# Attention scores as eight 64x32 matmuls a product instead of two of 64x128

## What is computed

```python
h = _layernorm(x) * (1 + ca) + sa
xh = h.reshape(1, 4096, 16, 16)                       # 16 heads of 16 features
q = einsum('bnhd,hed->bnhe', xh, Wq)
scores = einsum('bnhe,bmhe->bhnm', q, q) / NORM       # 4096 x 4096 per head
attn = softmax(scores, axis=-1)
res = einsum('bhnm,bmhe->bnhe', attn, q)
x = x + ga * (res.reshape(1, 4096, 256) @ Wp.T + bp)
h = _layernorm(x) * (1 + cb) + sb
x = x + gb * ffn(h)     # layernorm, 256 -> 1024, silu, 1024 -> 256, residual
```

## Time and profile before

| | before |
|---|---|
| median of 3 runs | 1982.75 us (1982.64 to 1982.96) |
| the profiled execution | 1984.1 us |
| its span (first to last instruction) | 1982.3 us |
| TensorE / ScalarE / VectorE / GpSimd busy | 94% / 95% / 75% / 68% |
| mean granted TensorE clock | 0.996 |

### The profile page before, as it was taken

One profiled execution on the slowest core, in us unless ns is written; L12 is line 12 of the kernel. 1 busy time (PEld: TensorE's weight loads), 2 busy tenths in 40 slices (PEclk: granted clock), 3 DMA queues, 4 the chain that ended last, 5 costly groups with the idle time before them and its releaser, 6 DMA issues.

```text
span 1982.3 us, 47924 instructions
## 1 busy us (share of the span) xinstructions
PE 1872.9 (94%) x18453; PEld 547.5 (28%) x18453; DVE 1482.4 (75%) x2599; ACT 1882.3 (95%) x1491; POOL 1353.1 (68%) x2265
## 2 busy tenths in 40 slices
PE   8787889999999999999999999999999999999999
PEld 6311112222222222222222222222222222322225
DVE  5578677778777777777777787777777777777763
ACT  5898999999999999999999999999999999999992
POOL 5277777478746787477774787557874777747870
PEclk9899999999999999999999999999999999999999
DMA  6531112112111222211212212111121121211100
GB/s 202 164 98 43 39 46 48 48 53 52 49 45 46 53 53 54 53 43 44 57 49 53 54 43 56 41 52 53 44 63 45 41 52 52 55 35 39 43 12 13
DMA packets 121394, 108.43 MB, mean 55 GB/s; under 512 B 21952, under 2 KB 120128, under 8 KB 120912
## 3 DMA queue, kind: packets, MB, share of 16 engines
q1 hardware_dynamic: 120416, 103.69, 19.6%
q10 hardware_dynamic: 752, 1.67, 0.2%
HBM read 96.49 MB, written 8.65 MB: 53 GB/s over the span
## 4 chain that ended last, share of the span: by engine, by line
PE 52%; ACT 28%; issue 8%; DVE 6%; POOL 3%; POOLq 0%; DVEq 0%
PE attend_sums L919 26%; ACT attend_probs L866 17%; PE attend_scores L905 15%; ACT attend_probs L872 10%; PE attend_out L927 8%; PE attend_scores L927 1%; DVE attend_spare L1123 1%; DVE attend_probs L1117 1%; DVE attend_probs L1116 1%; ACT hidden L860 1%; PE attend_out L933 1%; DVE attend_spare L1125 1%; PE attend_sums L933 0%; POOL attend_spare L832 0%; POOL attend_spare L834 0%
## 5 line engine op out<-in xcount | busy, mean ns | idle before, releaser
L866 ACT ACTIVATE attend_probs<-attend_scores 128x2048 f32<-128x2048 f32 x683 | 1287.1, 1884 | 21.5 <-PE attend_scores L905 20.9
L919 PE MATMUL attend_sums<-attend_probs,values 128*17 128x512 f32 x8192 | 1007.0, 597 | 14.6 <-DVE attend_att L1093 6.8
L1116 DVE COPY attend_probs<-attend_scores 128x896 f32<-128x896 f32 x620 | 675.3, 1089 | 345.1 <-PE attend_scores L905 340.3
L872 ACT ACTIVATE attend_probs<-attend_probs 128x896 f32<-128x896 f32 (+1 forms) x682 | 659.5, 967 | 12.3 <-DVE attend_probs L1116 11.2
L905 PE MATMUL attend_scores<-asks,keys 64*128 64x512 f16 x4096 | 565.3, 381 | 78.8 <-ACT attend_probs L866 70.5
L830 POOL TENSOR_TENSOR attend_spare<-attend_spare 128x256 f32<-128x256 f32 x310 | 204.2, 659 | 291.9 <-DVE attend_spare L1125 291.4
L905 PEld LDWEIGHTS attend_scores<-asks,keys 64*128 64x128 f16 x4096 | 149.2, 94 | 672.4 <-ACT attend_probs L866 514.0
L919 PEld LDWEIGHTS attend_sums<-attend_probs,values 128*17 128x17 f32 x8192 | 174.7, 96 | 522.4 <-issue 466.4
L834 POOL TENSOR_TENSOR attend_spare<-attend_spare 128x256 f32<-128x256 f32 x310 | 240.5, 776 | 25.8
L837 POOL TENSOR_TENSOR attend_spare<-attend_spare,attend_probs 128x256 f32<-128x256 f32 x310 | 227.6, 734 | 25.9
L839 POOL TENSOR_TENSOR attend_probs<-attend_spare 128x256 f32<-128x256 f32 x310 | 227.6, 734 | 24.3
(11 more groups left out here) (162 smaller groups left out, 834.8 us busy)
## 6 DMA issues: line engine op xcount, KB each, us to landing
keys<-parts_dram SPq DMA_DIRECT2D x768, 64.0 KB
keys<-parts_dram SPq DMA_DIRECT2D x256, 56.0 KB
asks<-parts_dram SPq DMA_DIRECT2D x192, 64.0 KB
start_x_in<-L_attn_x SPq DMA_DIRECT2D x8, 512.0 KB, 9.5
parts_dram<-start_q_parts SPq DMA_DIRECT2D x16, 256.0 KB, 2.7
attend_x_now<-L_attn_x SPq DMA_DIRECT2D x8, 512.0 KB, 4.4
out<-base SPq DMA_DIRECT2D x15, 256.0 KB, 2.6
asks<-parts_dram SPq DMA_DIRECT2D x64, 56.0 KB
```

Of the source, the lines that this page charges most:

```text
L866: act.activation(place(n, 2), ps_scores[:, 0:4, :], ACT.Exp, scale=scale).then_inc(exps_done, 1)
L872: act.activation(cols, cols, ACT.Exp, scale=scale).then_inc(exps_done, 1)
L919: last = pe.matmul(ps_sums[32 * hq:32 * hq + E1, :], values[:, j + STEPS * b, (gg % Q_GROUPS) * Q_HEADS + hq, :], place(gg * PAIRS + Q_HEA ...
L1116: dve.tensor_copy(flat(n, 0, DIRECT), bank[:, 0:DIRECT]).then_inc(copied, 1)
```

## The change

Each of the two matmuls of a product, with 64 rows and 128 columns, is made as four of 64 rows and 32 columns. Column tile q takes 32 of the 128 keys, and writes partitions 32q to 32q + 31 of the same PSUM bank. The four column tiles are the outer loop and the two row halves the inner one, so a product is eight matmuls in eight tiles. Waits, semaphores and everything else are unchanged, and so are the values that are written.

```diff
-                    for b in range(2):
-                        rows, col = slice(64 * b, 64 * b + 64), (j % K_STEPS) * P
-                        last = pe.matmul(ps_scores[:, 2 * i + b, :], keys[rows, part % K_RING, hq, col:col + P],
-                                         asks[rows, group * Q_HEADS + hq, :], start=True, stop=True)
+                    for q in range(4):
+                        for b in range(2):
+                            rows, col = slice(64 * b, 64 * b + 64), (j % K_STEPS) * P + 32 * q
+                            last = pe.matmul(ps_scores[32 * q:32 * q + 32, 2 * i + b, :], keys[rows, part % K_RING, hq, col:col + 32],
+                                             asks[rows, group * Q_HEADS + hq, :], start=True, stop=True)
                     last.then_inc(scores_ready, 1)
```

## The result

| | before | after |
|---|---|---|
| median us | 1982.7 (1982.45 to 1982.96, 4 runs) | 1996.65 (1995.37 to 1997.16, 4 runs) |
| ratio, 95% interval | 1 | 1.0069 (1.0052 to 1.0087) |
| the profiled execution: time, span | 1984.1, 1982.3 | 1995.37, 1993.6 |

The change made the kernel 14 us slower. The forecast was 33 us slower, 2016: the right way, inside the range, and more than twice too much.

The account below looks back on a forecast made before the run. ScalarE and TensorE bound the kernel in a loop of 2.61 us a round. Skew 0.04 plus later end 0.03, less 0.015 covered, times 626 rounds adds 34 us to 1984.1: 2016 us at the median, range 1962 to 2050.

Parts of the forecast that it names:

- The loop: Wide exp, two scores products, next wide exp: 2.61 us a round, to grow by 0.07, of which 0.015 is covered.
- point 1: Scores matmuls: row halves and column tiles were taken to overlap fully, so a product stays at 0.22 us.
- point 2: Inside a scores product: eight tiles start one after another, so the last starts 0.04 us later.
- point 3: Scores to their reader: column tiles finish 0.03 us later than recorded.
- point 4: TensorE's switches between scores and sums: stops of 0.09 and 0.12 us, 0.23 us a round in all, were taken to stay.
- Rival 1: The stops go because only columns count; TensorE's round becomes 2.44 us, the time 1971 us; chance 0.29.
- point 5: Fetching 24,576 more instructions, some 4.1 MB in the queue, costs nothing because it is hidden behind matmuls.
- The tanh rounds: The 56 rounds with a tanh between the exps: 3.12 us each, with 0.5 us to spare against a later product.
- The sum: Loop growth of 0.07 us, less 0.015 covered, gives 0.055 in each of 626 rounds: 34 us.

Follow-up runs that it names:

- third_product_second: Kernel before, with the third product made between the first and second in 640 of 683 rounds, same matmuls; 2055.69 us, 1.0364 of the kernel before.
- two_column_tiles: Each scores product made as four matmuls in tiles of 64 x 64, where the kernel before has two; 1990.53 us, 1.0035 of the kernel before.
- one_shape_at_a_time: Kernel before plus four extra fp16 matmuls a round, tiles varied so type, rows and columns change one at a time; 2181.55 us beside 1983.44.
- split_queries: Each scores product made as eight matmuls of 64 rows x 128 columns over 128 queries, without column tiles; 1990.57 us, 1.0037 of the kernel before.
- half_outer: The change with its loops exchanged, row half outer and column tile inner; 1995.47 us, 1.0066 of the kernel before.

## Why the prediction was right in kind and wrong in size

- *The loop.* Right: it sets the round of the change, and third_product_second, which ends the second product 0.2 later with the same instructions, has a round 0.19 longer. The 0.015 us of cover stood in the forecast without a working; by the parts above the loop of before is 2.58 and the cover is 0.02. TensorE's own round was said to grow by the same 0.07, in step with the loop; it grew by 0.02, to 2.611 or 2.617, since only the skew is in it.
- *Streaming* (point 1). Right: eight tiles of 64 x 32 stream together, and products start 0.22 to 0.23 apart.
- *Skew* (point 2). This step failed: 0.04 was taken, 0.02 measured. I took the 0.006 a step from the fp32 column tiles; the row halves' 0.003 to 0.004, the lower bound in the text, was the right row. (The 0.045 of the upper end has no row; by point 2 it is 0.042 less 0.004, and the bound some 4 us lower.)
- *The later end* (point 3). Right: 0.03 (0.441 against 0.412 from the last matmul to its reader), and two_column_tiles shows that it grows with the column tiles. The two rows that it was taken from have different readers, ScalarE and VectorE; with ScalarE as the reader of both (line 506's, and line 882) it is 0.037 and 0.067, the same 0.03.
- *The stops* (point 4). Right that they stay, and one_shape_at_a_time shows that a change of rows alone is enough, which the forecast could only argue. Rival 1 is out.
- *Instructions* (point 5). Right in the fetching: 4.01 MB where 4.1 was said. That so many cost nothing is not shown: split_queries, with as many, loses half of what the change loses, by a TensorE round that is 0.02 longer.
- *The tanh rounds.* A tanh round was read as 3.12 us with 0.5 to spare. The trace of before has a median of 3.43 us for the 56: in 33 of them TensorE has 16 sums and 8 matmuls of line 927, and ScalarE waits for it (fence below). So these had nothing to spare, and the 56 together paid 1.4 us.
- *The sum.* This step failed too, and it is the larger lesson. It added 0.055 us to each of 626 rounds. But a longer loop is a floor under the round, not an addition to it: a round that was already longer pays nothing until the floor reaches it. Of the 626 rounds without a tanh in the trace of before, 454 were shorter than 2.63 us. Raising just these to 2.63 gives 11.9 us; measured in the profiles are 11.5 us in the rounds without a tanh and 1.4 in those with one, together the 12.9 above. Round by round, these 454 got 12.5 us longer from before to after and the 172 others 1.0 shorter. With the forecast's own floor of 2.655 the same count gives 23 us instead of 34. So of the 22 us too much in the profile (34 against 12), some 11 are the sum, and some 11 the floor that was 0.025 too high, of which the skew is 0.02 and the cover 0.005. By the same count TensorE's own round of 2.611 to 2.617 would by itself have cost 4 to 6 us (an estimate); the loop made it 12.

The tanh round of the earlier trace rows, from its wide exp to the next, in ScalarE's timeline of before:

```profile
1084.64 1.90 ACT L866 ACTIVATE attend_probs<-attend_scores 128x2048 f32<-128x2048 f32 x1
...
1088.09 1.88 ACT L866 ACTIVATE attend_probs<-attend_scores 128x2048 f32<-128x2048 f32 x1 [0.20 <-PE attend_scores L905]
```

The count by floors, with each kernel's median round as the floor, holds for the other kernels: split_queries 6.9 us against 5.9 measured in its rounds without a tanh, two_column_tiles 5.6 against 7.2, half_outer 11.9 against 11.1. Only where the floor is high does it say too much: third_product_second 98 against 72. There 41 of the 626 rounds keep the old order (7 us), and the rounds that had been longer became shorter: what stands over 2.80 us fell from 22 us in before to 9. TensorE waits 0.20 us in the usual round there, so it has time to work off a backlog; that this is the reason was not tested. So lost time did come back, which the forecast had put at next to nothing; at the change's own floor it is within the error of the count. What the remaining 40 us over the floor of 2.63 are made of was not taken apart.

No run here beats the kernel before: each way of cutting a product makes its last matmul start or end later, and none gets back the 0.23 us of stops. A kernel whose scores and sums have the same rows and columns was not run.

## What to carry to other kernels

Before cutting a matmul into tiles to please the array, look for the reader that waits for the last of them: here a cut that keeps the pace of streaming cost 0.05 us in the loop from exp to scores to exp, and the loop had 0.02 to spare. Then look at the engine itself: the same cut made TensorE's own round 0.02 longer, and in the milder variants that was what set the time. Which of two engines waits for the other, at both ends of the loop, tells which chain is the floor. Treat a lengthened loop as a floor: count the rounds that lie under it, from the starts in the trace, and don't multiply by all of them. To save the stop between two kinds of matmul, rows and columns must both agree: in these rows a change of either alone cost as much as a change of both, and a change of type next to nothing.

## What was unexpected in the hardware

- The end of a product reaches its reader later the more column tiles it has: 0.412 us from the start of its last matmul with one tile of 128 columns, 0.422 with two of 64, 0.441 with four of 32. Two row halves add next to nothing: their reader starts 0.036 us behind the recorded end, and that of one whole fp32 tile 0.037 (line 506; the shortest of each). Why column tiles end later is not shown.
- fp16 tiles of 64 x 32 start 0.003 us apart, whether the row half or the column tile changes from one to the next (0.004 at times); fp32 tiles of 128 x 17 start 0.006 to 0.007 apart.
- A change from fp32 to fp16 within one tile shape costs at most 0.02 us, where a change of rows or of columns costs 0.10 to 0.11.
- Twenty-four matmuls with 24 loads ran in 0.84 us in each round, of which the last one's own time is 0.38, and the products kept the 0.22 us of before. With loads of 128 columns for each 128 queries (split_queries) they started 0.007 us further apart.
